# Depth attention: hand-overs by pairs of heads, and the norms' clip as a reduction

## The reference, cut to what matters

```python
def l2norm(t):
    return t / jnp.clip(jnp.linalg.norm(t, axis=-1, keepdims=True), 1e-12)
...
q = l2norm(q) * qs
k = l2norm(k) * ksc
q, k = rotary_xpos(q, k)
...
sim = jnp.einsum('bhwid,bhwjd->bhwij', bq, bk)
sim = jnp.where(mask, -jnp.finfo(sim.dtype).max, sim)
attn = jax.nn.softmax(sim, axis=-1)
out = jnp.einsum('bhwij,bhwjd->bhwid', attn, bv)
```

## Time and profile before

| | |
|---|---|
| median of 3 runs | 2039.09 us (2038.13 to 2039.49) |
| the profiled execution, its own time | 2050.75 us |
| its span | 2049.0 us |
| busy: PE, DVE, ACT, POOL | 1809.1, 1283.5, 1039.6, 699.8 us |
| mean granted clock of TensorE | 0.961 of full speed |
| attention of depth layer 0, of depth layer 1 | about 948 to 1207 us, 1322 to 1588 us of the span |

### The profile page before, as it was taken

How to read it: one execution, slowest core, us unless ns; L and a number is a source line. 1 busy time by engine, 2 the same in 40 slices (tenths; PEclk the granted TensorE clock), 3 DMA queues, 4 the chain that set the end, 5 groups by cost and what they waited for, 6 DMA issues and landing times. The chain is left out here.

```text
span 2049.0 us, 32327 instructions
## 1 busy us (share of the span) xinstructions
PE 1809.1 (88%) x11428; PEld 1167.7 (57%) x11428; DVE 1283.5 (63%) x2721; ACT 1039.6 (51%) x2198; POOL 699.8 (34%) x1001
## 2 busy tenths in 40 slices
PE   6989999999899797997999989999998998871895
PEld 3445555555576465664666655566666554550795
DVE  5589999999523584234787852368877344957112
ACT  3489999999412263222767631257675112640232
POOL 0023333333424344232555521045554112540312
PEclk9999999999999899998999999999999999985897
DMA  3441111110000200021000010010000000055695
GB/s 118 145 145 43 43 43 43 43 43 2 1 1 0 62 1 1 0 63 44 1 6 6 6 53 16 1 44 6 4 4 6 20 1 16 1 160 133 184 312 163
DMA packets 104896, 101.72 MB, mean 50 GB/s; under 512 B 34896, under 2 KB 88480, under 8 KB 104608
## 3 DMA queue, kind: packets, MB, share of 16 engines
q1 hardware_dynamic: 101664, 95.31, 15.8%
q0 software_dynamic: 3072, 4.34, 1.2%
HBM read 80.60 MB, written 16.92 MB: 48 GB/s over the span
## 5 line engine op out<-in xcount | busy, mean ns | idle before, releaser
L612 DVE TENSOR_REDUCE negmax<-sps 128x1 f32<-128x1024 f32 x256 | 309.1, 1218 | 17.5 <-PE sps L534 13.0
L656 ACT ACTIVATE prob<-sps,negmax 128x1024 f32<-128x1024 f32 x256 | 285.7, 1117 | 23.7 <-DVE negmax L612 19.1
L1531 POOL TENSOR_TENSOR la_pr<-la_pr,la_ri 128x512 f32<-128x512 f32 x128 | 157.3, 1257 | 160.7 <-DVE la_ri L1594 160.7
L702 POOL TENSOR_TENSOR probT<-probT,after 128x128 f32<-128x128 f32 x256 | 117.4, 458 | 237.6 <-DVE probT L620 211.8
L1781 ACT ACTIVATE la_pr<-la_pr,la_nx 128x256 f32<-128x256 f32 x256 | 126.5, 495 | 127.8 <-DVE la_nx L1635 127.8
L534 PE MATMUL sps<-ks,qs 128*128 128x512 f16 x512 | 170.1, 384 | 7.7 <-PEq L42 3.1
L1966 PE MATMUL la_bs<-lf_zT,lfw 128*128 128x512 f32 x352 | 153.0, 594 | 0.0
L550 PE MATMUL tps<-ident,prob 128*128 128x128 f32 x704 | 125.4, 282 | 22.7 <-DVE probT L620 20.3
L1541 POOL TENSOR_TENSOR la_qs<-la_qn,ores 128x256 f32<-128x256 f32 x128 | 113.9, 922 | 88.8 <-DVE la_qn L1648 88.8
L550 PEld LDWEIGHTS tps<-ident,prob 128*128 128x128 f32 x704 | 79.7, 141 | 89.3 <-issue 43.8
L1966 PEld LDWEIGHTS la_bs<-lf_zT,lfw 128*128 128x128 f32 x352 | 66.4, 190 | 82.5 <-issue 82.3
(11 more groups left out here) (378 smaller groups left out, 3899.9 us busy)
## 6 DMA issues: line engine op xcount, KB each, us to landing
w1e<-in_fc_T SPq DMA_DIRECT2D x16, 1024.0 KB, 5.9
w2e<-in_fc_T SPq DMA_DIRECT2D x16, 1024.0 KB, 8.9
qs<-q_parts SPq DMA_DIRECT2D x128, 64.0 KB, 2.0
ks<-k_parts SPq DMA_DIRECT2D x128, 64.0 KB, 1.9
q_parts<-parts SPq DMA_DIRECT2D x8, 512.0 KB, 3.6
k_parts<-parts SPq DMA_DIRECT2D x8, 512.0 KB, 3.6
lfw<-in_L_ffn_w SPq DMA_DIRECT2D x6, 640.0 KB
ores<-in_L_ffn_wqkv SPq DMA_DIRECT2D x2, 1536.0 KB, 6.5
```

The costliest lines, as they stand in the source:

```text
L612: dve.tensor_reduce(negmax[:, n % 4:n % 4 + 1], slots[n % NS][:], X, ALU.max, negate=True).then_inc(s.max_done, 1)
L656: act.activation(prob[:, n % 3, :], slots[n % NS][:], ACT.Exp, bias=negmax[:, n % 4:n % 4 + 1], accum_out=rowsum[:, tile % 2, n % QUAD:n % ...
L702: pool.tensor_tensor(blk, blk, after[:], ALU.mult).then_inc(s.masked, 1)
L1531: ins = pool.tensor_tensor(prob[:, h:h + 2, :], prob[:, h:h + 2, :], rinv[:, h:h + 2].unsqueeze(2).to_broadcast([P, 2, 2 * P]), ALU.mult)
```

## The change

It does two things.

First, `max_done`, `exp_done` and `rinv_done` are raised per pair of heads, four times a tile instead of two. ACT waits for the maxima of each pair, DVE computes four reciprocals of 2 sums each instead of two of 4, each behind its own wait, and POOL waits in front of each of its four multiplications. `scaled`, for which TensorE waits, stays at two per tile. The order of the work in each list is the same.

Second, the clip `max(norm, 1e-12)` was a tensor_scalar on 16 norms; now `norm` has a second column that holds 1e-12, written once by POOL at the start, ACT writes its roots into the first column, and DVE takes the maximum over the two columns with a tensor_reduce.

```diff
-                norm = sb("la_nm", [P, 2 * HL], F32, c)
+                norm = sb("la_nm", [P, 2 * HL, 2], F32, c)
...
+                        pool.memset(norm[:, :, 1], 1e-12).then_inc(s.floors, 1)
...
                         def scale(t):
                             for half in range(2):
-                                pool.wait_ge(s.rinv_done, 2 * t + half + 1)
                                 for n in range(2):
                                     h = half * HL // 2 + 2 * n
+                                    pool.wait_ge(s.rinv_done, 4 * t + 2 * half + n + 1)
                                     ins = pool.tensor_tensor(prob[:, h:h + 2, :], prob[:, h:h + 2, :],
...
                         def inverse(t, half):
-                            dve.wait_ge(s.exp_done, 2 * t + half + 1)
                             if t > 0:
                                 dve.wait_ge(s.scaled, 2 * t - 1 + half)
-                            at = slice(half * HL // 2, (half + 1) * HL // 2)
-                            dve.reciprocal(rinv[:, at], rsum[:, at]).then_inc(s.rinv_done, 1)
+                            for n in range(2):
+                                h = half * HL // 2 + 2 * n
+                                dve.wait_ge(s.exp_done, 4 * t + 2 * half + n + 1)
+                                dve.reciprocal(rinv[:, h:h + 2], rsum[:, h:h + 2]).then_inc(s.rinv_done, 1)
...
                                                                    1.0, FAR, ALU.add, ALU.min, nmax[:, h:h + 1])
-                                ins.then_inc(s.max_done, 1)
+                                    if h % 2:
+                                        ins.then_inc(s.max_done, 1)
...
                             dve.wait_ge(s.norm_done, t + 1)
-                            dve.tensor_scalar(rnorm[:], norm[:], 1e-12, None, ALU.max).then_inc(s.clipped, 1)
+                            if t == 0 and l == 0:
+                                dve.wait_ge(s.floors, 1)
+                            dve.tensor_reduce(rnorm[:], norm[:], X, ALU.max).then_inc(s.clipped, 1)
...
-                            act.activation(norm[:], ssum[:], ACT.Sqrt).then_inc(s.norm_done, 1)
+                            act.activation(norm[:, :, 0], ssum[:], ACT.Sqrt).then_inc(s.norm_done, 1)
...
                         def exponents(t):
                             if t > 0:
-                                act.wait_ge(s.rinv_done, 2 * t)
-                            for half in range(2):
-                                act.wait_ge(s.max_done, 2 * t + half + 1)
-                                for h in heads(half):
+                                act.wait_ge(s.rinv_done, 4 * t)
+                            for two in range(HL // 2):
+                                act.wait_ge(s.max_done, 4 * t + two + 1)
+                                for h in (2 * two, 2 * two + 1):
                                     ins = act.activation(prob[:, h, :], prob[:, h, :], ACT.Exp, scale=-1.0,
                                                          bias=nmax[:, h:h + 1], accum_out=rsum[:, h:h + 1])
                                 ins.then_inc(s.exp_done, 1)
```

More of the change, by code:

```diff
@@ L1455, in depth_layers @@
                 p3 = [bqk[:, 512 * i:512 * i + 512].rearrange("p (a d) -> p a d", a=2) for i in range(2)]
-                sa = [signals(f"la{l}", "@tables_in @edges @built1 @built2 @tab1 @x_turned @h_done @qk_done "
+                sa = [signals(f"la{l}", "@tables_in @edges @floors @built1 @built2 @tab1 @x_turned @h_done @qk_done "
                             "@squared @ssum_done @norm_done @clipped @rnorm_done @normed @cos_done @sin_done "
```

## The result

The changed kernel took 2009.81 us in the median of 4 runs (2008.07 to 2012.67), the kernel before 2038.61 beside it: ratio 0.9857, 95% interval 0.9844 to 0.9870, so 28.8 us or 1.4% faster.

The account below looks back on a forecast made before the run. TensorE's work was taken to bound the depth attention's turns, with two waits above it. Middle turns 16.5, first turns 2.1 and last two turns 3.2 us sum to 21.8 off the 2039.09 median: 2017.3 us, range 2013.5 to 2025.

Parts of the forecast that it names:

- TensorE's two waits bound the turn, and the change frees them: Middle turns of the depth attention: waits at L1851 and L1873, 0.19 and 0.36 us in one turn, would both go.
- The turn is bound by TensorE's work, and everything above 14.19 us is these two waits: Middle turns of 14.74 and 14.94 us: TensorE busy 14.19 us in both, only the waits at L1851 and L1873 removable.
- the term of the middle turns: Waits at L1851 and L1873 in 13 middle turns of each layer: 16.5 us saved in all.
- The first turns: First turn of each layer: shorter waits at L1851 and L1873, together 2.1 us saved.
- The last two turns: Last two turns of each layer, paced by the softmax chain: each ends 0.8 us sooner with POOL, 3.2 us in all.
- The lower end of the range: Whole kernel's time: 2013.5 us, if shorter waits in the last turns keep the clock up.
- The clock's gift: Last turns: shorter waits keep TensorE's clock up, at most the 2.9 us lost there in each layer, 2014.
- The clip: Norm chain: tensor_reduce takes 0.21 us against 0.76; L1873's wait goes, as it would with the maxima by pairs alone.
- Two more reciprocals cost nothing on the path: DVE, each turn: two extra reciprocals of 0.10 us each, in a place where DVE has just won 0.83 us.
- Rival 1: Middle turns: POOL starts first, `rotary_sum` waits for two multiplications; gain 2.6 us less, 2020; chance 0.08.
- Rivals 2 to 4: 2: POOL's multiplications stretch, 2028, 0.12; 3: waits return where TensorE next meets DVE, 2039, 0.05; 4: only chance 0.03 given.

Follow-up runs that it names:

- e9: The kernel before, unchanged, profiled again to catch one of its shorter executions: 2039.81 us.
- e1: The changed kernel with the clip put back to tensor_scalar, so the pairs alone: ratio 0.9868 to the kernel before.
- e3: The changed kernel with reciprocals again two of four sums, only the maxima by pairs: ratio 0.9856 to the kernel before.
- e8: The kernel before, unchanged, profiled a second time: 2050.51 us.
- the first profile: The kernel before, unchanged, in the profile that the prediction was read from: 2050.75 us.

## Why the prediction was right in its steps and wrong in its size

- *TensorE's two waits bound the turn, and the change frees them.* Right: no wait row is left in 26 turns, and each hand-over moved to within 0.1 us of where it was put (exponents, clip, product, POOL's end).
- *"The turn is bound by TensorE's work, and everything above 14.19 us is these two waits."* This is the step that failed. 14.19 us was TensorE's busy time, and the prediction took that for work which no change in the waits would touch. Each of the two waits held 0.22 us of it. A matmul's row is longer than its share of a sequence: 8 transposes show 1.04 to 1.09 us, and 16 without a wait 1.91, not 2.1. Where the next group follows at once its start lies over the tail of the last; behind a wait it doesn't, and the tail counts as busy. The page "TensorE: Matmul & The Clock Gate" of the Trainium skill, Step-by-step: what each phase is for, says that the drain of one matmul overlaps the fill of the next. It says nothing of waits; the rows agree in so far as 0.16 us of overlap is lost at each. In the sum the term of the middle turns, 16.5 us, should have been that plus 0.2 for each of 52 waits: 16.5 + 10.4 = 26.9; it measured 27.6, which is 0.21 for each. This one term is 11.1 us too small; all the others together came out 2.1 us less than forecast (the first turns 0.5, the last 0.2, everything else 1.4).
- *The first turns, 2.1 us.* 1.6. In layer 1 the wait of 0.90 us at the second half of L1851 stayed (0.91 after), and in layer 0 one of 0.55 is left at L1878. In the 13th turn of each layer the 16 transposes take longer, a wait too short for a row (in layer 0 0.12 us idle in the window 1157.27 to 1159.35):

```profile
1157.27 2.25 PE L1856 MATMUL la_bs<-ident,la_pr 128*128 128x128 f32 x16
```

- *The last two turns, 3.2 us.* 3.0, but split by luck: 0.7 in layer 0 and 2.3 in layer 1, for 1.6 each. The idle rows ahead of L1856 did shorten by 0.9 us each (4.21 and 2.41 before, 3.33 and 1.48 after, in both layers); that is 1.8 us a layer. In layer 0 a row of 0.9 us between the halves of L1856 is new in both turns, and the granted clock is 0.89 (1160 to 1192 us), as in both layers of e9; in layer 1 it is 0.94 (1525 to 1554). What share the clock has in it is not shown.
- *The lower end of the range.* The clock's gift was put at 2.9 us "in each layer" and the time at 2014. Two layers are 5.8 us and make 2011.5; 2014 is one layer's. The measured 2009.81 lies below either.
- *The clip.* Forecast 0.21 us with bounds of 0.175 and 0.24; 0.185 to 0.188 in all 32 turns. That it is redundant at L1873 beside the pairs was nearly right: alone, the pairs leave 0.12 to 0.33 us a turn (e1), since TensorE comes to L1873 at T+9.69 and not at T+10.07.
- *Two more reciprocals cost nothing on the path.* Right; e3 shows that they bring nothing either. The maxima keep DVE busy until T+2.76, and by T+2.95 ACT has the sums of all four heads of the first half: a pair's reciprocal can gain at most 0.2 us.
- *Rival 1 came true without its price.* POOL does start ahead of `rotary_sum` now, and DVE waits: 2.03 us for 1.23, one multiplication and not the two of the rival. The slack took all of it: e3, with 1.23, has the same turn.
- Rivals 2 to 4: POOL's four take 5.02 us (4.97 before), so 2 is out; no new wait row stands in the middle turns, and they got shorter, so 3 is out; TensorE's clock was 1.00 in all middle turns, so 4 is out.

## What to carry to other kernels

Count a recurring short wait of TensorE at its idle row plus about 0.2 us (measured here between groups of float32 transposes and matmuls), and don't take a busy time that was measured with waits in it for the floor: compare starts of the same group in a stretch with the wait and one without. When an engine's hand-over is split finer, find the consumer that stood idle for it (here ACT, for the maxima): here the split of the reciprocals brought nothing once that one was made. A tiny elementwise instruction whose duration swings between 0.18 and 0.8 us is waiting for something that no wait row names; one of another kind may not.

## What the runs showed of the hardware

- *An instruction of DVE and one of POOL take turns, whole.* Before, `rotary_sum` started 0.15 us ahead of POOL's first multiplication, ran 1.23 us, and the multiplication took 1975 ns. After, POOL starts 0.09 us ahead, its first takes 1042 ns, and `rotary_sum` 2.03; the second multiplication then takes 2021 (L1532 in the window 1044.5 to 1045):

```profile
L1532 POOL TENSOR_TENSOR la_pr<-la_pr,la_ri x1: 2021/2021/2021, 1043.9 to 1043.9; 128x512 f32<-128x512 f32 x1
```

  Both read two tensors of SBUF. "SBUF — State Buffer" of the Trainium skill, Who interferes with whom, has this: issue order decides who blocks.
- *The clip as a tensor_reduce is not held up by POOL*: 185 to 188 ns in 32 turns, beside 175 to 811 for the tensor_scalar.
- *One program has executions 10 us apart* (2037 to 2042 us and 2049 to 2052 for the kernel before, side by side), with a mean granted clock of 0.963 to 0.967 and of 0.958 to 0.960. The place of the longer low stretches differs: 5.6 us of e8 against e9 lie in the ends of the two layers, 8.9 us of the first profile behind them. What starts the low stretch at one time and not at another stays open.
